# An attention kernel on one core: scores, pairs of maxima and exponentials get banks of their own

## The reference

```python
# convolution block
x  = group_norm(hidden) + pos_emb
w  = sigmoid(conv1x1(silu(conv3x3(silu(conv1x1(x))))))      # spatial gate
sh = group_norm(x) as tokens                                # 1024 x 128
standard = softmax(q k^T / 4) v            # 8 heads of 16, q, k, v from sh
multi    = two more attentions of width 64 # q from x * w, k and v from sh
final    = group_norm(out(ff2(silu(ff1([standard, multi]))))) + hidden
# token block
t = t + attention(layer_norm(t))           # 8 heads of 16
t = t + experts(layer_norm(t))             # 8 experts of width 512, the best two of each token
```

## Time and profile before

| | |
|---|---|
| median of 3 runs | 3164.26 us (3162.4 to 3170.27) |
| the profiled execution | 3157.17 us, span 3155.4 us |
| mean granted TensorE clock | 0.922 |

### The profile page before, as it was taken

One profiled execution on the slowest core, in us unless ns is written; L12 is line 12 of the kernel. 1 busy time (PEld: TensorE's weight loads), 2 busy tenths in 40 slices (PEclk: granted clock), 3 DMA queues, 4 the chain that ended last, 5 costly groups with the idle time before them and its releaser, 6 DMA issues. The chain is left out here.

```text
span 3155.4 us, 40976 instructions
## 1 busy us (share of the span) xinstructions
PE 2572.8 (82%) x15040; PEld 1002.1 (32%) x15040; DVE 2121.8 (67%) x3208; ACT 1679.8 (53%) x2454; POOL 631.2 (20%) x539
## 2 busy tenths in 40 slices
PE   3686888988789887998789887898888988898745
PEld 1122222352125322262223621253222622236134
DVE  4756868577775877667685777758776687766520
ACT  1452555556565565556555565654655556555613
POOL 4000122015110240104220151102401032101222
PEclk9997889998999999998889998998989989899967
DMA  4002310273014430163102730145301542017024
GB/s 110 2 1 47 63 20 13 82 183 78 1 41 137 110 68 1 54 196 79 26 15 80 184 77 1 32 137 118 68 1 54 178 85 38 9 63 197 22 83 143
DMA packets 155340, 228.87 MB, mean 73 GB/s; under 512 B 24544, under 2 KB 72576, under 8 KB 155056
## 3 DMA queue, kind: packets, MB, share of 16 engines
q1 hardware_dynamic: 146992, 209.76, 26.6%
q0 software_dynamic: 8192, 16.79, 1.8%
HBM read 174.28 MB, written 52.20 MB: 72 GB/s over the span
## 5 line engine op out<-in xcount | busy, mean ns | idle before, releaser
L1416 DVE TENSOR_REDUCE blockmax<-ps 128x2 f32<-128x1024 f32 x1152 | 1357.1, 1221 | 445.2 <-PE ps L780 364.0
L1237 ACT ACTIVATE prob<-ps 128x1024 f32<-128x1024 f32 x1024 | 1016.1, 1023 | 695.6 <-PE ps L964 691.6
L964 PE MATMUL ps<-qs,ks 99*128 99x512 bf16 x2048 | 631.1, 408 | 319.0 <-DVE blockmax L1416 259.4
L964 PEld LDWEIGHTS ps<-qs,ks 99*128 99x128 bf16 x2048 | 152.3, 101 | 689.2 <-DVE blockmax L1416 454.0
L614 POOL TENSOR_TENSOR rs<-vn,vec 128x1 f32<-128x1 f32 (+1 forms) x40 | 40.1, 1004 | 1614.8 <-DVE vn L1362 1117.6
L981 PE MATMUL ps<-prob,va_b 128*32 128x512 f32 x1984 | 301.6, 683 | 0.0
L1285 ACT ACTIVATE prob<-ps,b1t 128x128 f32<-128x128 f32 x736 | 209.8, 368 | 164.6 <-PE ps L1076 164.4
L981 PE MATMUL ps<-prob,va_a 128*32 128x512 f32 x2048 | 291.1, 642 | 0.0
L1263 ACT ACTIVATE prob<-ps 128x1024 f32<-128x1024 f32 x128 | 130.1, 1023 | 160.0 <-PE ps L1033 92.5
L657 POOL DMA_INDIRECT x_dram<-ta,slot_u x128 | 124.0, 969 | 345.6 <-DVE slot_u L1643 309.0
L625 POOL DMA_INDIRECT routed<-y_dram,slot_u x128 | 127.8, 999 | 133.5 <-DMA y_dram<-prob 96.6
(11 more groups left out here) (243 smaller groups left out, 3243.8 us busy)
## 6 DMA issues: line engine op xcount, KB each, us to landing
parts_dram<-parts SPq DMA_DIRECT2D x32, 768.0 KB, 4.8
ks<-parts_dram SPq DMA_DIRECT2D x192, 128.0 KB, 4.8
qs<-parts_dram SPq DMA_DIRECT2D x192, 128.0 KB, 6.6
shared<-in_w SPq DMA_DIRECT2D x96, 256.0 KB, 3.3
prob<-in_w SPq DMA_DIRECT2D x96, 256.0 KB, 3.2
routed<-in_w SPq DMA_DIRECT2D x80, 256.0 KB, 3.4
xe<-in_w SPq DMA_DIRECT2D x48, 256.0 KB, 3.4
oatt<-in_w SPq DMA_DIRECT2D x48, 256.0 KB, 3.1
```

Source lines behind the costliest of these rows:

```text
L964: mm = pe.matmul(slot_banks(n + pr)[:, j, :], ks[:, slot_of(a, g), h, t * P:(t + 1) * P], qs[:, slot_of(a, g), h, cols(q)], start=True, st ...
L1237: act.activation(prob[:, n % 3, 2 * pr:2 * pr + 2, :], slot_banks(n + pr), ACT.Exp, scale=HD ** -0.5).then_inc(exp_done[a], 1)
L1416: dve.tensor_reduce(cells, banks, AX.X, ALU.max).then_inc(blocks_used[f], 1)
```

## The change

- Scores: one bank for each head, banks 0 and 1 in turn; four exponentials of one head each in place of two of two heads. The scores of heads 2 and 3 stand behind the weighting of the values in TensorE's order.
- Pairs: banks 2 and 3 for the first pair of a step, 6 and 7 for the second, each waiting for the reduction of the same pair of the step before.
- Turns stand behind the pairs like other small products; several small products move by a step.
- The rows of maxima go from SBUF straight into `qs` (or `mrow`), one DMA for each of the three rows; `qs` is laid out by half, head, query, and its spread takes two DMAs where there was one.
- 24 pairs of a token attention in the expert stage instead of 22, from slot 13; the front of the next image keeps 22 (`FRONT`), one step earlier, so that the last step has no pairs.
- The layer norm of the experts' tokens moves from VectorE to GpSimd, the copy of the gates (`trg`) and the second group norm's `xh` from VectorE to ScalarE.
- Three products that nobody reads follow the token attention on TensorE.

The core of the diff:

```diff
+FRONT = 22
+EARLY = 24
-assert TOKEN_PAIR_STEPS + EARLY // STEP_PAIRS == 2 * STEPS
+assert TOKEN_PAIR_STEPS + FRONT_PAIR_STEPS == 2 * STEPS - 1
...
-CONV_EXTRA = {6: ["stats_e0"], 7: ["stats_e1"], 8: ["aggr_e"], 9: ["norm_e0"], 10: ["norm_e1"], 15: ["find0"],
-              16: ["find1"], 17: ["routes"], 19: ["slots_k"], 20: ["slots_e"], 22: ["gates"], 30: ["biases"]}
+CONV_EXTRA = {6: ["stats_e0"], 7: ["stats_e1"], 8: ["aggr_e"], 15: ["find0"], 16: ["find1"], 17: ["routes"],
+              20: ["slots_k"], 22: ["slots_e"], 23: ["gates"], 30: ["biases"]}
...
-TOKEN_WINDOW = {1: ["pre"], 5: ["turn_b_1"], 6: ["norm"], 9: ["kA0"], 10: ["kA1"], 11: ["qA0"], 12: ["qA1"],
-                13: ["turn_b_2"], 14: ["vA0"], 15: ["vA1"], 16: ["c10"], 17: ["c11"], 18: ["vm0"], 19: ["vm1"],
-                20: ["res0"], 21: ["turn_b_3"], 22: ["res1"], 24: ["c2"], 26: ["c30"], 28: ["c31"],
-                29: ["turn_a0_0"]}
+TOKEN_WINDOW = {1: ["pre"], 4: ["turn_b_1"], 6: ["norm"], 9: ["kA0"], 10: ["kA1"], 11: ["qA0"], 12: ["turn_b_2"],
+                13: ["qA1"], 14: ["vA0"], 15: ["vA1"], 16: ["c10"], 17: ["c11"], 18: ["vm0"], 19: ["vm1"],
+                20: ["turn_b_3"], 21: ["res0"], 22: ["res1"], 24: ["c2"], 26: ["c30"], 27: ["c31"],
+                28: ["turn_a0_0"]}
...
-PAIR_SLOT = 14
+PAIR_SLOT = 13
...
+def early_pairs(s):
+
+    return {PAIR_SLOT: range(0, 1), PAIR_SLOT + 1: range(1, 4)}.get(
+        s, range(SLOT_PAIRS * (s - PAIR_SLOT), SLOT_PAIRS * (s - PAIR_SLOT + 1)) if s > PAIR_SLOT else ())
...
-        qs = sb("qs", [ROWS + 3, 3, GH, S], BF16)
+        qs = sb("qs", [ROWS + 3, 3, 2, GH, HALF], BF16)
...
-        def slot_banks(i):
-
-            first = (SC, SC + 2, MX)[i % 3]
+        def pair_banks(i):
+
+            first = (SC + 2, MX)[i]
             return ps[:, first:first + 2, :]
...
+                        for q in range(2):
+                            sp.dma_start(qs[rows, slot_of(a, g), q, :, :], src[:, :, cols(q)]).then_inc(spread[a][g], 16)
...
-                sp.dma_start(maxrow_dram[a, u].rearrange("r c s -> c r s"), maxrow[:, u % 2, :, :]).then_inc(rows_out[f], 16)
-                sp.wait_ge(rows_out[f], 16 * n)
...
+                for c in range(3):
+                    if u < 4:
+                        sp.dma_start(qs[ROWS + c:ROWS + c + 1, slot_of(a, u // 2), u % 2, :, :], maxrow[:, u % 2, c, :]
+                                     ).then_inc(rows_in[f], 16)
+                        continue
...
+                for t in range(NT):
+                    pool.tensor_scalar(lnt[:, t, :], toke[:, t, :], rs[:, t:t + 1], nb[:, t:t + 1], ALU.mult, ALU.add
+                                       ).then_inc(done["ln_e"], 1)
...
             def max_pair(a, n, i, f, d, run):
 
-                if i == 0 and n:
-                    pairs_used(a, n - 1)
-                elif i == 0 and a == 1 and run:
+                if n:
+                    pair_used(a, n - 1, i)
+                elif i == 1 and a == 1:
                     pe.wait_ge(blocks_used["b"], EARLY)
-                elif i == 1 and run:
-                    pe.wait_ge(exp_done[a], 2 * n + 1)
-                banks = slot_banks(n + 2 + i)
...
+                banks = pair_banks(i)
...
-            def scores(a, n, pr):
+            def scores(a, n, h):
...
+                if GH * n + h >= 2:
+                    pe.wait_ge(exp_done[a], GH * n + h - 1)
...
+                pe.matmul(ps[:, SC + h % 2, :], ks[:, slot_of(a, g), h, t * P:(t + 1) * P],
+                          qs[:, slot_of(a, g), q, h, :], start=True, stop=True).then_inc(scores_ready[a], 1)
...
+            def unread_products(count):
+
+                pe.wait_ge(blocks_used["a0"], FRONT)
+                for _ in range(count):
+                    pe.matmul(pair_banks(0)[:, 0, :], one_b[:, :], parts[:, 1, 0, 0:HALF], start=True, stop=True)
+
             def attention_step(a, n, pairs, run, names):
...
-                for name in names:
-                    if name.startswith("turn"):
-                        small_product(name)
+                if run:
+                    scores(a, n, 2)
+                    scores(a, n, 3)
                 for i, (f, d) in enumerate(pairs):
                     max_pair(a, n, i, f, d, run)
...
+            def normalize():
+
+                act.wait_ge(done["norm_coefs"], 1)
+                act.activation(xh[:, :], x1[:, :], ACT.Identity, bias=cb[:, :], scale=ca[:, :]).then_inc(done["xh_a"], 1)
...
-                for pr in range(2):
-                    act.wait_ge(scores_ready[a], 2 * n + pr + 1)
-                    act.activation(prob[:, n % 3, 2 * pr:2 * pr + 2, :], slot_banks(n + pr), ACT.Exp, scale=HD ** -0.5
+                for h in range(GH):
+                    act.wait_ge(scores_ready[a], GH * n + h + 1)
+                    act.activation(prob[:, n % 3, h, :], ps[:, SC + h % 2, :], ACT.Exp, scale=HD ** -0.5
                                    ).then_inc(exp_done[a], 1)
...
+                    if token and front and n == 8:
+                        normalize()
...
             def start_xh():
                 group_coefs("norm")
-                dve.tensor_scalar(xh[:, :], x1[:, :], ca[:, :], cb[:, :], ALU.mult, ALU.add
-                                  ).then_inc(done["xh_a"], 1)
+                dve.sem_inc(done["norm_coefs"], 1)
```

More of the change, by code:

```diff
@@ L119, in conv_pairs @@
 def conv_pairs(n):
-    first = EARLY + STEP_PAIRS * n
+    first = FRONT + STEP_PAIRS * n
     return [("a1", d) for d in range(first, first + STEP_PAIRS)] if n < CONV_PAIR_STEPS else []
 def token_pairs(n, token, front):
-    first = EARLY + STEP_PAIRS * n
     if n < TOKEN_PAIR_STEPS:
+        first = EARLY + STEP_PAIRS * n
         return [("b", d) for d in range(first, first + STEP_PAIRS)] if token else []
-    return [("a0", d - HEAD_PAIRS) for d in range(first, first + STEP_PAIRS)] if front else []
+    first = STEP_PAIRS * (n - TOKEN_PAIR_STEPS)
+    return [("a0", d) for d in range(first, first + STEP_PAIRS)] if front and first < FRONT else []
+def early_pairs(s):
+    return {PAIR_SLOT: range(0, 1), PAIR_SLOT + 1: range(1, 4)}.get(
+        s, range(SLOT_PAIRS * (s - PAIR_SLOT), SLOT_PAIRS * (s - PAIR_SLOT + 1)) if s > PAIR_SLOT else ())
 def unit_of(d):
@@ L474, in spread_group @@
                     for j in range(count):
-                        dst = (ks, qs)[i][HD * (first + j):HD * (first + j + 1), slot_of(a, g), :, :]
-                        src = parts_dram[a, i, :, (j, run)[i], :].rearrange("(h two d) s -> two d h s", two=2, d=HD)
-                        sp.dma_start(dst, src[g]).then_inc(spread[a][g], 16)
+                        rows = slice(HD * (first + j), HD * (first + j + 1))
+                        src = parts_dram[a, i, :, (j, run)[i], :].rearrange("(h two d) s -> two d h s", two=2, d=HD)[g]
+                        if i == 0:
+                            sp.dma_start(ks[rows, slot_of(a, g), :, :], src).then_inc(spread[a][g], 16)
+                            continue
+                        for q in range(2):
+                            sp.dma_start(qs[rows, slot_of(a, g), q, :, :], src[:, :, cols(q)]).then_inc(spread[a][g], 16)
             def spread_max(f, u):
@@ L908, in small_product @@
                     h = int(name[2:])
-                    pe.wait_ge(done["gate_t"], 1 + h)
+                    pe.wait_ge(small_free, small[f"trg{h}"])
                     for t in range(4):
@@ L1008, in attention_step @@
                 for name in names:
-                    if not name.startswith("turn"):
-                        small_product(name)
+                    small_product(name)
             if experts or conv:
@@ L1104, in tensor_program @@
                     if token and s >= PAIR_SLOT:
-                        for i in range(SLOT_PAIRS):
-                            d = SLOT_PAIRS * (s - PAIR_SLOT) + i
+                        for d in early_pairs(s):
                             early_pair(d)
@@ L1120, in tensor_program @@
                     attention_step(1, n, token_pairs(n, token, front), token, small.token.get(n, ()))
+                if token and front:
+                    unread_products(3)
         def scalar_program(act, conv, experts, token, front, small):
@@ L1302, in scalar_program @@
             if front or token:
+                if not token:
+                    normalize()
                 for n in range(2 * STEPS):
+                    if token and front and n == 8:
+                        normalize()
                     if token:
@@ L1702, in attention_step @@
             def attention_step(n, pairs, names, extra):
+                for i, (f, d) in enumerate(pairs):
+                    reduce_pair(f, d, pair_banks(i))
                 for name in names:
-                    if name.startswith("turn"):
-                        small_product(name)
-                for i, (f, d) in enumerate(pairs):
-                    reduce_pair(f, d, slot_banks(n + 2 + i))
-                for name in names:
```

(3 more changed lines are left out.)

132 lines of the change are left out of this document (55 added, 77 removed).

## The result

The changed kernel takes 3019.91 us (median of 4 executions, 3017.48 to 3021.3); the kernel before took 3167.27 beside it. The ratio is 0.9532, interval 0.9511 to 0.9553: faster by 147 us where the sum had promised 186. The profiled execution took 3020.56 us, 137 less than that of before, with a span of 3018.8 and a mean granted clock of 0.950.

The account below looks back on a forecast made before the run. No engine was always busy: reductions and exponentials shared banks in a ring, each waiting for the other through TensorE's order. Terms summed to -186 from the profiled 3157.2, giving 2971, plus 7 for the median: 2978 us, range 2880 to 3075.

Parts of the forecast that it names:

- convolution blocks with experts: Seven convolution blocks with expert work: each falls from 116.6 to 103 us with VectorE as the pace, -95 in all.
- token blocks: Seven token blocks: each falls from 121.6 to 111 us through shorter steps and moved turns, -74 in all.
- Banks and exponentials: Attention steps: separate banks remove waits between scores and reductions; exponentials take 0.60, a plain pair step 2.9 instead of 3.24.
- The 97 us: Exponentials on ScalarE: four short ones cost 97 us more over 512 steps if ScalarE set the pace; not charged.
- Rows of maxima: Rows sent straight into the operand: one hop in place of two, nothing waits for either, so no gain.
- ScalarE idles 40%: Attention blocks: ScalarE's idle time was the reason to charge nothing for the skill's dearer short exponentials.
- VectorE as the pace of the convolution block: Convolution block with experts: VectorE's remaining 92.2 us set the length, 3.25 a pair step, busy for nine tenths.
- Turns: Turns of maxima behind their step's pairs: reductions go first, 6 us off a token block, bounds 0 and 4 x 3.8.
- xh: Token step 8: ScalarE waits for VectorE's coefficients; 3.4 charged plus 0.6 for a lower clock, bounds 0 and 5.5.
- Block end: End of a token block: pairs end a step earlier, so the exponential ends it; -1.6 each, -11 over seven.
- Two more pairs: Expert stage between convolution and token block: two more pairs cost up to 2.4 an image, half hidden, +8.
- Rival 3, the clock: TensorE's short stops bring the lower clock level; with a third of 512 steps so, 3270 us; chance 0.07.

Follow-up runs that it names:

- one_exp_ring: Kernel before, each exponential of two heads split into two of one head, ring of banks, order and waits kept: 3165.37 us, ratio 1.0013.
- rows_first: Changed kernel, rows of maxima of a token attention's third unit queued ahead of the store and the next image's key copies: 3011.2 us, ratio 0.953.
- halves_pool: Changed kernel, second bfloat16 copy of the wide keys and queries made by GpSimd from the first copy instead of by ScalarE: 3000.34 us, ratio 0.9495.
- norm_vector: Changed kernel, layer norm of the experts' tokens back on VectorE at steps 9 and 10 of the convolution block: 3041.89 us, ratio 0.9619.
- turns_first: Changed kernel, turns of maxima again ahead of the pairs of their step on TensorE and VectorE: 3091.74 us, ratio 0.9783.
- turns_split: Changed kernel, turns of maxima ahead of the pairs again and the split's remainder kept in PSUM: 3064.27 us, ratio 0.97.
- wide_rows: Changed kernel, wide attentions' rows of maxima sent by three DMAs instead of six, TensorE's wait moved behind two products not using them: 3006.81 us, ratio 0.9522.

## Why the prediction came out as it did

By the two profiled executions, these are the terms of the sum (first exponential to last, times the number of blocks):

```
                                   forecast   measured
convolution blocks with experts      -95        -78
token blocks                         -74        -38
token block to next block            -11        -25
first convolution block              -10         -7
last token block                      -4         -5
convolution to token block            +8        +18
before the first exponential           0         -4
after the last                         0         +2
sum                                 -186       -137
```

- *The size of the whole: in part luck.* The forecast subtracted its new lengths, 103 and 111, from one block of each kind, 116.6 and 121.6; the means of seven are 118.9 and 123.9. Against these the same new lengths would have given 32 us more. So the convolution block came out 4.7 too long and the token block 7.5, 85 us in all, of which the short blocks of before hide 32.
- *Banks and exponentials: right in the plain step.* Exponential 0.60 (0.596), plain step 2.9 (2.88), the waits where they were expected, and one_exp_ring shows that the split alone gains nothing. No run takes the banks or the order of the scores back, so their part of the 147 us isn't measured. Taken back one at a time, turns, layer norm and unread products cost 79, 27 and 23 us. The Trainium skill's 186 ns and 0.833 ns an element (ScalarE: Activation LUTs, What ACT_TABLE_LOAD costs) give, as an estimate, 0.61 for such an instruction; the row agrees (0.596). The 97 us, the prediction's estimate from these figures for a ScalarE that sets the pace, didn't come in one_exp_ring, the same split in the old ring (ratio 1.0013).
- *"Rows of maxima ... nothing waits for either in these rows, so nothing": the step that failed.* The kernel before already waited for them. In the block of the earlier trace rows its trace has the second hop on the queue, and TensorE behind it:

```profile
1120.55 0.70 SPq L487 DMA_DIRECT2D qs<-maxrow_dram  x1
```

```profile
1122.84 1.04 PE L964 MATMUL ps<-qs,ks 99*128 99x512 bf16 x4 [0.39 <-DMA qs<-maxrow_dram]
```

  In all seven blocks this wait is 0.29 to 0.70 us. So the rows had no time to spare, and their reader moved further than they did: in the mean TensorE reached these scores 63.5 us into the block before and 60.1 now, and got the rows at 63.9 and at 62.5, a wait of 0.5 and of 2.4. The stop and the lower clock behind it cost 5.2 us a block, by steps 15 and 16 of rows_first: 36 us, as much as the token blocks' gain fell short of the forecast. rows_first adds that the stop can't simply be booked as a loss: removed, it let the split run into GpSimd.
- *"That ScalarE idles 40% of these stretches is why I charge nothing for it".* True of the exponentials, wrong of its reads of small products. With the product between the pairs and the next scores, each read lies on the chain: a step takes 3.50 with one read (token steps 10 and 11, forecast 3.25) and 3.93 with two. halves_pool takes 2.3 of the 4.7 us by which a convolution block missed 103.
- *VectorE as the pace of the convolution block.* It is busy for 92.4 us, as summed (92.2), so the layer norm on GpSimd cost it nothing that shows. But that is 85% of 108.6 and not nine tenths: norm_vector passes on half of what it adds, halves_pool gains without touching VectorE.
- *Turns: mechanism right, undersized.* The forecast was 6 us a token block; turns_first puts 7.5 there (10.1 without the late rows) and 2.8 in the convolution block, and turns_split shows that the stretched split of the earlier trace rows is 7.3 of it in the token block.
- *`xh`: right.* 4.0 us were charged; step 7 is 4.3 longer than a plain step, and a later place gives 4.0 a block back.
- *Block end.* The forecast was -1.6 each, and -3.6 was measured. "I put no gain on them", of the unread products, was wrong: they are worth 23 us.
- *Two more pairs, and rows of the wide attentions.* Of the 18 us more from convolution to token block, the wide rows' wait is 0.6 a block; at full clock the stretch takes 120.8 with wide_rows and 120.04 before, so the two pairs and the rest of the change cost at most 0.8 a block. What is left is mostly the lower clock, which this stretch meets more often now.
- *Rival 3, the clock,* went the other way in the mean (0.922 to 0.950). But in the experiments it decides where a saving stays.

## What to carry to other kernels

When the steps ahead get shorter, everything that must arrive in a step comes due earlier: list each arrival (DMAs behind others on a queue, coefficients, bank releases) with the time to spare that it has now, and charge it where the step's gain is larger. An engine that idles 40% can still be on the chain, if what it reads stands between two links of it. And removing one stop of several microseconds is worth less than its length, until the next thing that is late has been found: here the split beside GpSimd, and behind it the next unit's rows.

## What the runs showed of the hardware that was not expected

- VectorE's small operations wait out an elementwise GpSimd operation beside them when input and output (the cast) or both inputs (the subtraction) are in SBUF (0.21 to 0.90, 0.28 to 1.38 and up to 2.23), and not when they read PSUM (at most 0.29 in 288 operations). Who begins first decides: in the kernels before and after, in rows_first and in turns_first, every such operation that began while one of GpSimd's ran ended behind it, a cast by 0.07 to 0.08 us and a subtraction by 0.14 to 0.15; seven subtractions in turns_first that began 0.07 ahead of GpSimd's took their 0.28. Beside GpSimd's indirect copies the same operations took 0.45 at most.
- A strip of TensorE work can be the same to 0.01 us and be followed by either clock. Convolution step 14 takes 4.68 us in the changed kernel and in rows_first, with TensorE busy for 4.58 and 4.57 at full clock, 16 short products of 1.95 us in it. Step 15 by stretches, in the changed kernel and in rows_first:

```profile
834.04:838.08 4.04, 4.04 (x27) 1.10 (x26) 3.42 (x12) 3.14 (x7) 0.00 (x0) 1.00 0.03 6
```

```profile
1182.35:1187.94 5.59, 5.59 (x27) 1.26 (x26) 3.64 (x12) 3.14 (x6) 0.00 (x0) 0.69 0.02 4
```

  It is so in none of the seven blocks of the one and in all seven of the other. What decides it was not found; it moves 1.5 us a block, some 11 us in all, between kernels that differ elsewhere.
- Three short products that nobody reads, at the end of a block, are worth 23 us, give or take 11: with them the next block's first step has the full clock in six of seven blocks, without them in none.
